# Second layer of a four-layer chain: GpSimd's low part of the inputs waits for VectorE's low temporal sum, the last four state matmul groups are issued together, the output is scaled ahead of the input gate

## The reference, cut to what matters

```
ctx      = causal_ema(x, tau_ctx)
gated    = x * sigmoid(Wg @ [x, ctx] + bg)
h1       = gelu(Wn1 @ x + bn1)
mod      = 0.5 + sigmoid(Wn2 @ h1 + bn2)                 # one column per trace
traces_d = causal_ema(gated * mod_d, tau_d)              # 32 traces
temporal = sum_d softmax(blend)_d * traces_d
gate     = sigmoid(Wtemp @ temporal + btemp)
soma     = gelu(Wsoma @ x + bsoma)
out      = Wout @ (soma * gate)
x        = x + layernorm(out) * gamma + beta
```

## Time and profile before

| what | value |
|---|---|
| median of 3 runs (2167.59 to 2168.61) | 2168.57 us |
| the profiled execution's own time | 2169.59 us |
| its span, first to last instruction | 2167.9 us |
| mean granted TensorE clock | 0.973 of full |
| busy share PE / PEld / DVE / ACT / POOL | 92% / 75% / 75% / 56% / 36% |
| the second layer's bodies 1 to 31 | from 994.64 us to some 1640 us of the span |
| one body in the steady part | 20.63 us |
| granted TensorE clock in that body | 1.00 of full |

### The profile page before, as it was taken

The page is one execution under the profiler, slowest core; times in us unless marked ns, Lnnn a source line. Parts: engine busy times, 40 slices in busy tenths (PEclk is TensorE's granted clock), DMA queues, the critical chain, the costliest instruction groups (busy, mean ns, idle before and its releaser), DMA issues. The chain is left out here.

```text
span 2167.9 us, 42832 instructions
## 1 busy us (share of the span) xinstructions
PE 1993.4 (92%) x14158; PEld 1630.0 (75%) x14158; DVE 1620.8 (75%) x2498; ACT 1220.5 (56%) x2588; POOL 776.8 (36%) x589
## 2 busy tenths in 40 slices
PE   3899999999999999939999999999995999999998
PEld 2566666666666666628888788888875999999997
DVE  6788888888888888857777777777763666666664
ACT  1466666666666666534665665656654555555553
POOL 4644444444444444133333433433320111111111
PEclk8999999999999999969999999999997999999998
DMA  3444444444444444210000000000002222222221
GB/s 94 108 109 107 107 107 107 107 107 107 107 107 107 107 107 107 55 29 1 1 0 0 0 0 0 0 0 0 0 0 88 69 71 87 65 87 66 86 70 59
DMA packets 121175, 137.52 MB, mean 63 GB/s; under 512 B 24240, under 2 KB 89776, under 8 KB 121136
## 3 DMA queue, kind: packets, MB, share of 16 engines
q1 hardware_dynamic: 118576, 128.64, 23.1%
q0 software_dynamic: 2560, 8.39, 1.0%
HBM read 48.35 MB, written 8.39 MB: 26 GB/s over the span
## 5 line engine op out<-in xcount | busy, mean ns | idle before, releaser
L366 DVE TENSOR_REDUCE a_neg_max<-a_s 128x2 f32<-128x512 f32 x512 | 328.9, 682 | 122.8 <-PE a_s L613 121.4
L487 ACT ACTIVATE a_e<-a_t 128x512 f32<-128x512 f32 x512 | 281.1, 610 | 228.1 <-PE a_t L626 228.1
L375 DVE SCALAR_TENSOR_TENSOR a_e<-a_e,a_w_t 128x1024 f32<-128x1024 f32 x256 | 373.3, 1467 | 4.0 <-ACT a_e L487 4.0
L613 PE MATMUL a_s<-a_k_st,a_q_st 96*128 96x256 f32 x1024 | 274.8, 379 | 0.0
L898 POOL TENSOR_TENSOR b_decayed<-b_table,b_mod_t 128x1024 f32<-128x1024 f32 x64 | 127.1, 2007 | 270.6 <-ACT b_mod_t L1169 263.3
L613 PEld LDWEIGHTS a_s<-a_k_st,a_q_st 96*128 96x128 f32 x1024 | 203.2, 198 | 13.5
L1705 ACT ACTIVATE c_hid<-c_pH,c_b 128x256 f32<-128x256 f32 x256 | 107.7, 472 | 187.8 <-PE c_pH L1768 187.3
L610 PE MATMUL a_s<-a_add_m,ident_bf 128*128 128x512 bf16 x512 | 201.5, 394 | 8.0 <-POOL a_add_m L254 5.9
L1329 PE MATMUL b_pS<-b_gated_t,b_decayed 128*128 128x256 f32 x768 | 188.7, 389 | 1.2
L626 PE MATMUL a_t<-a_q_st,a_k_st 97*128 97x512 f32 x512 | 177.2, 427 | 2.8 <-DMA a_q_st<-a_max_row 2.0
L642 PE MATMUL a_v<-a_e,a_v_pad 128*32 128x256 f32 x2048 | 163.4, 392 | 4.5 <-DVE a_e L375 2.1
(11 more groups left out here) (262 smaller groups left out, 5629.4 us busy)
## 6 DMA issues: line engine op xcount, KB each, us to landing
a_q_st<-a_q_hi SPq DMA_DIRECT2D x256, 128.0 KB, 2.4
a_k_st<-a_k_hi SPq DMA_DIRECT2D x256, 64.0 KB, 2.0
a_q_st<-a_q_lo SPq DMA_DIRECT2D x128, 128.0 KB, 2.4
a_xs<-in_xT SPq DMA_DIRECT2D x32, 256.0 KB, 2.8
a_k_st<-a_k_lo SPq DMA_DIRECT2D x128, 64.0 KB, 2.1
x_all<-in_xT SPq DMA_DIRECT2D x32, 256.0 KB, 2.7
c_we<-in_we SPq DMA_DIRECT2D x32, 256.0 KB, 2.7
c_key_t<-in_keyT SPq DMA_DIRECT2D x32, 256.0 KB, 3.1
```

Of the source, the lines that this page charges most:

```text
L366: dve.tensor_reduce(neg_max[:, qc, head:head + 2], ps_s[b][:], AX.X, ALU.max, negate=True).then_inc(red_done, 1)
L375: dve.scalar_tensor_tensor(out=buf[:], in0=buf[:], scalar=BIG, in1=w_t[par][:, kc].unsqueeze(1).to_broadcast([P, 4, S]), op0=ALU.min, op1= ...
L487: act.activation(e[g % E_BUFS][:, 2 * b:2 * b + 2], ps_t[b][:], ACT.Exp).then_inc(exp_done, 1)
L613: ins = pe.matmul(ps_s[b][:, r], q_st[par][0:96, slot, qc * P:qc * P + P], k_st[par][0:96, slot // 2], start=False, stop=(r == 1))
```

## The change

On POOL, `low_x` gets one more wait: for entry n it waits until n-1 `low_temporal` have been made, so that in a body it comes behind DVE's `low_temporal` of that body. On PE, `states(n, par, 3)` is moved up to stand right behind `states(n, par, 2)`, and `turn_normed` is moved ahead of `lags(n, par, 7)`. On DVE, `states(n, 2)` and `states(n, 3)` both stand ahead of `lag_sum(n, par, 4)`. On ACT, `normalized(n - 1)` stands ahead of `input_gate(n + 1)`. No instruction is added or taken away but the wait.

```diff
@@ gpsimd @@
         def low_x(n, par):
             pool.wait_ge(xhi_done, n + 1)
+            at_least(pool, templo_done, n - 1)
             pool.tensor_tensor(x_p[par][1][:], xn(n), x_p[par][0][:].bitcast(F32), ALU.subtract).then_inc(xlo_done, 1)
@@ vector, body @@
+            states(n, 2)
+            states(n, 3)
             lag_sum(n, par, 4)
-            states(n, 2)
             if has_c:
                 norm(n - 1)
             lag_sum(n, par, 5)
-            states(n, 3)
             if has_a:
                 gating(n + 1, 1 - par)
@@ scalar, body @@
             if has_c:
                 deviation(n - 1)
+                normalized(n - 1)
             if has_a:
                 input_gate(n + 1)
-            if has_c:
-                normalized(n - 1)
             spread_out(n)
@@ tensor, body @@
             states(n, par, 2)
+            states(n, par, 3)
             lags(n, par, 4)
             if has_a:
                 gate_in(n + 1, 1 - par, 1)
             lags(n, par, 5)
-            states(n, par, 3)
             lags(n, par, 6)
             spread(n, 1)
-            lags(n, par, 7)
             if has_c:
                 turn_normed(n - 1)
+            lags(n, par, 7)
             soma_in(n, par)
```

## The result

The changed kernel took 2131.68 us in the median (2129.90 to 2131.89, 4 runs) against 2168.59 (4 runs): a ratio of 0.9829, 95% interval 0.9812 to 0.9846. That is 36.9 us less, 2132 was forecast. The first matmul of the third layer starts at 1623.3 us where it started at 1661.0, so all of the difference arises ahead of the third layer. From the first `turn_back` of the layer to its last it is 601.1 us where it was 637.1: 36.0 less in 31 bodies, and the rest of the 37.7 arises ahead of the first (1.3) and behind the last (0.4).

What follows compares the result with a forecast made beforehand. PE was taken to bound the kernel, standing still at two waits in each body. Gains of 23.4 and 13.6 us, together 37 off 2169.59, and 1.0 for the median gave 2131.6, stated as 2132, range 2119 to 2148.

Steps and rivals of the forecast that it cites:

- The first wait: PE's `gate_out` loses 1.16 us waiting for DVE's low temporal sum; moving `low_x` behind it regains 0.90.
- `low_x` late for `hidden`: `low_x`, moved later on POOL, ends just in time for PE's `hidden`: 0.10 us charged, bounds 0 and 0.4.
- The second wait: PE's `spread` 1 loses 0.80 us waiting for the fourth state product; grouping the states removes it.
- the second half: From the start of `states` 2 to the next `turn_back`: 0.80 - 0.07 = 0.73 us in 32 bodies, 23.4 us.
- the state groups: PE's two groups take 1.62 and 1.54 us, so `lags` 4 starts 3.16 behind the start of `states` 2.
- The reciprocal and `turn_normed`: DVE's reciprocal stands 5.09 us behind `states` 2, held by `decays`; PE's `turn_normed` waits 0.07, bounds 0 and 0.4.
- The last addition and `residual`: POOL's `residual` comes first by 0.15 us, DVE's last addition waits it out, `total` is late: 0.33 goes back.
- The sum: 23.4 us from second halves and 13.6 from first halves, together 37 off the profiled execution, giving 2132.
- the first halves: From `turn_back` to the start of `states` 2: 0.90 - 0.33 - 0.10 = 0.47 us in 29 bodies, 13.6 us.
- The order that would have given 2122: Rival: DVE's last addition slips in ahead of `residual`, so the first half gains 0.80; chance 0.20.
- The meeting of `low_context` and the low temporal sum: Rival: `low_context` on POOL still overlaps DVE's sum, first half gains nothing, 2145; chance 0.14, shared with late `low_x`.
- The slower case: Rival: DVE's state products contend with POOL's `low_x` and `decays`, +0.9 us a body, some 2196; chance 0.04.

Runs made afterwards that it cites:

- the eighth experiment: Changed kernel with the reciprocal ahead of lag 4, plus lags 4 between the two state groups on TensorE: 2123.33 us, ratio 0.9784.
- the fourth experiment: Changed kernel with VectorE's reciprocal (`norm`) moved ahead of `lag_sum` 4: 2122.30 us, ratio 0.9780; again 2122.58 us.
- fifth experiment: Changed kernel with GpSimd's `residual` also waiting for VectorE's last addition of the lags: 2130.90 us, ratio 0.9821.
- the second experiment: Changed kernel without GpSimd's new wait, the rest of the change kept: 2152.93 us, ratio 0.9920 to the kernel before.
- the sixth: Changed kernel with `turn_normed` behind lags 7 again on TensorE: 2132.52 us, ratio 0.9826.

## Why the prediction was right, point by point

**The first wait.** Right. The low temporal sum takes 0.686 where 0.68 was taken, and alone the wait on POOL gave 26.5 us; 0.90 less 0.08 in 29 bodies had given 24.

**`low_x` late for `hidden`.** Charged 0.10, measured 0.07 to 0.08 (G to S 7.14 to 7.21 in the body shown; `hidden`'s first row is 0.33 long where it was 0.28). `low_x` ends at 1307.82 and `hidden` starts at 1307.88.

**The second wait.** The mechanism was right and the size off: 0.80 was put on it, and the second half gained 0.63 of the 0.73 forecast. The term that was mis-sized is that of the state groups: `lags` 4 was to start at S+3.16, the sum of 1.62 and 1.54, and it starts at S+3.34. A `lags` that stands right behind state matmuls takes 0.42 to the next start, one that stands elsewhere 0.24; the first row is from the kernel before, where the row ahead of it is the `lags` at 1315.80, the other two are from the changed kernel:

```profile
1316.22 0.28 PE L1279 MATMUL b_pA<-b_x_hi,b_wg_hi 128*128 128x256 f32 x1
```
```profile
1308.63 0.40 PE L1356 MATMUL b_pL<-b_mod_st,b_w_st 96*128 96x256 f32 x2
1308.87 0.28 PE L1279 MATMUL b_pA<-b_x_hi,b_wg_hi 128*128 128x256 f32 x1
```

By the modelled ends the state matmuls run to 1316.15, 0.35 into that `lags`. What stands right behind them pays some 0.18: in the sixteen rows it is the second group. Where `lags` 6 stood behind them in the kernel before, it lay hidden in the wait of `spread` 1, which was therefore worth 0.62 and not 0.80; the 0.34 that the prediction took for `lags` 6 was read from `lags` 7, which has no state matmuls ahead of it. The parted groups of the eighth experiment show that the place of this cost doesn't matter. Of the 0.18, `spread` 1 has all (S+5.77, forecast 5.59) and T has 0.10 left (S+8.97, forecast 8.87): 0.02 is the smaller wait of `turn_normed`, and why the stretch from there to T is 0.06 shorter than before is open.

**The reciprocal and `turn_normed`.** The reciprocal starts at S+5.22 (1318.76), forecast 5.09, late by 0.13. The fourth state product is late by the same 0.18 (S+3.73), and the addition of lag 4 with it; but that addition doesn't wait POOL's `decays` out, as the prediction had it. They end at S+4.50 and not at S+4.88 (3.63 us long, where they took 4.00 with additions beside them), ahead of its start at S+4.88. `turn_normed` waits 0.05, forecast 0.07 (0.62 behind the spread, which takes 0.57). The input gate ends at S+6.98, forecast 6.88.

**The last addition and `residual`.** This step decides the size of the result and was right: POOL came first, by 0.07 and 0.17 in turn where 0.15 was forecast; the addition ended 0.16 after POOL, as forecast, and `total` came at S+10.03, forecast 10.0. In the body shown the addition starts at S+8.63, exactly as forecast, and `residual` at S+8.56, 0.08 late, as every step of ACT from `normalized` on is late by 0.06 to 0.09. In the bodies between, `gating` starts 0.11 later and the addition with it. Because T itself came 0.10 later than forecast, `total` is 0.26 behind what PE alone would allow instead of 0.33. The Trainium skill's rule ("SBUF — State Buffer", section "SBUF: two separate sides": an exclusive lock for a whole instruction) agrees with the trace: 64 elements took 1.36 us, and half the bandwidth would have made them at most 0.6.

**The sum.** The forecast had 13.6 us in the first halves and 23.4 in the second, together 37.0. The trace has 17.8 from T to S in 31 bodies and 18.2 from S to T, and with the 1.3 and 0.4 at the two ends 19.9 for the second, together 37.7. So the split was 4 us off, and the sum 0.7. Most of this cancelling is no luck: in the changed kernel the length of a body is S to `total`, `total` to G and G to S, forecast 10.0, 2.19 and 7.24, measured 10.03, 2.14 (2.21 in the bodies between) and 7.21, and T is in none of them. An error in T moves time from one half to the other and costs nothing. What remains was luck of some hundredths of a us: POOL's `residual` came 0.08 late, and `total` followed the addition by 0.04 where 0.09 was taken. The counts of bodies were approximate as well: the last but one has no `low_x` and gains nothing up to G, and its second half takes 9.19 where it took 8.39.

**The rivals.** The order that would have given 2122 didn't come by itself; the fourth experiment made it, by moving the reciprocal, and took 2122.30. The meeting of `low_context` and the low temporal sum is real when `residual` is late (fifth experiment) and wasn't in the changed kernel. The slower case had no part: the two state products beside `low_x` take 1.28 us together, and took 1.27 before, in the rows of DVE at 1306.19 and 1306.91:

```profile
1306.19 1.28 DVE L1020 TENSOR_TENSOR b_state<-b_pS,b_w_rep 128x512 f32<-128x512 f32 x2
```
```profile
1306.91 1.27 DVE L1019 TENSOR_TENSOR b_state<-b_pS,b_w_rep 128x512 f32<-128x512 f32 x2
```

The first is the changed kernel with `low_x` from 1306.52 to 1307.82 beside it, the second the kernel before. Here a product with one input in PSUM isn't held.

**What stays open.** Why `gating` starts 0.11 later in every other body wasn't followed up, and the 0.20 to 0.27 that remain at `gate_out` with the early reciprocal were only shifted, not won.

## What to carry to other kernels

When an engine's instruction is long in some of its places and short in others, look which engine runs beside it before looking at the instruction: here the wait that moved one GpSimd instruction by some 1.1 us gave 26.5 us by itself. After moving one such pair apart, list every other pair of the two engines with its distance (here 0.96 us became less than nothing) and see who comes first; a tiny instruction on a chain, here a reciprocal of 0.16 us, is the place to win that distance back. And a wait of the bounding engine is worth what its start shows only if the group ahead of it leaves no tail behind: read the tail from a place where the same group is followed without a wait.

## What the runs showed of the hardware that I had not expected

A VectorE addition of 64 elements a partition, 0.29 us by itself, took 1.25 to 1.41 us whenever it started inside GpSimd's `residual` of 1.27 us, and ended 0.15 to 0.16 us after it: 29 of 32 bodies of the changed kernel, 30 in the second experiment, 28 in the sixth. In one body of the changed kernel both start at the same time, and there it is GpSimd's instruction that is longer, by 0.15:

```profile
1574.24 0.29 DVE L1037 TENSOR_TENSOR b_inner<-b_inner,b_prod 128x64 f32<-128x64 f32 x1
```
```profile
1574.24 1.43 POOL L904 TENSOR_TENSOR x_all<-b_wsoma,x_all 128x512 f32<-128x512 f32 x1 [3.99 <-ACT b_wsoma L1218]
```

The GpSimd instruction queued right behind `residual` was longer too: `low_context` was 1.34 to 1.36 us long there, and 1.28 to 1.31 where no such addition stood in its way.

A group of matmuls right behind eight rows of state matmuls took 0.41 or 0.42 us to the next start where it takes 0.24 elsewhere. A wait behind it hides this, so that start times alone put the wait too high: 0.80 was read, and the second half of a body gained 0.63.
